# Layer 0's query and key maxima carried through the pairs as one sequence of steps, half a pair ahead

## What is computed

```python
q = (x @ Wq).reshape(B, Nq, HEADS, DIM_HEAD)
k = (context @ Wk).reshape(B, context.shape[1], HEADS, DIM_HEAD)
v = (context @ Wv).reshape(B, context.shape[1], HEADS, DIM_HEAD)
sim = jnp.einsum('bihd,bjhd->bhij', q, k) * SCALE
attn = jax.nn.softmax(sim, axis=-1)
out = jnp.einsum('bhij,bjhd->bihd', attn, v)
...
x = _layernorm(x + _L0_xattn_ref(x, ctx_768, ...), axis=-1)
```

## Time and profile before

| | us |
|---|---|
| median of 3 runs | 1639.53 (1639.24 to 1639.96) |
| the profiled execution | 1638.51 |
| its span | 1636.8 |
| maxima ahead of the pairs, first matmul to the reduction | 59.6 to 125.1 |
| half 0, seeds to seeds | 126.8 to 234.8 |
| half 1 | 234.8 to 358.9 |
| half 2 | 358.9 to 466.3 |
| half 6 | 821.6 to 912.1 |
| mean granted clock of TensorE | 0.964 |

### The profile page before, as it was taken

The page is one execution under the profiler, slowest core; times in us unless marked ns, Lnnn a source line. Parts: engine busy times, 40 slices in busy tenths (PEclk is TensorE's granted clock), DMA queues, the critical chain, the costliest instruction groups (busy, mean ns, idle before and its releaser), DMA issues.

```text
span 1636.8 us, 27033 instructions
## 1 busy us (share of the span) xinstructions
PE 1530.1 (93%) x9058; PEld 548.9 (34%) x9058; DVE 1286.3 (79%) x2319; ACT 1126.0 (69%) x1541; POOL 490.9 (30%) x488
## 2 busy tenths in 40 slices
PE   6889999999999999999999998899997979999986
PEld 4312333333333333333333223344444612222223
DVE  6898987879977779878789897877775666787766
ACT  6787777768877778777777786655554469676643
POOL 6303343334543334433300010345451012233100
PEclk9759999999999999999999998999999979999998
DMA  4000000000200000000010000111100000000000
GB/s 135 7 1 11 1 1 1 1 2 11 54 1 2 1 1 1 3 1 11 20 32 3 1 1 19 37 46 45 45 27 1 1 1 2 0 1 1 1 14 13
DMA packets 14834, 22.79 MB, mean 14 GB/s; under 512 B 1990, under 2 KB 11766, under 8 KB 14710
## 3 DMA queue, kind: packets, MB, share of 16 engines
q1 hardware_dynamic: 14710, 21.22, 4.6%
HBM read 20.69 MB, written 0.52 MB: 13 GB/s over the span
## 4 chain that ended last, share of the span: by engine, by line
PE 69%; issue 11%; DVE 9%; POOL 5%; ACT 4%; DMA 0%; POOLq 0%; SPq 0%; DVEq 0%; ACTq 0%
PE PS L2167 22%; PE PS L2153 15%; PE PS L2511 6%; PE PS L2199 5%; POOL WRK L734 5%; PE PS L2498 3%; DVE KNB L1382 3%; PE PS L2020 2%; PE PS L2012 2%; PE PS L2116 2%; PE PS L2540 2%; PE PS L2450 1%; PE PS L2435 1%; PE PS L2004 1%; ACT KNB L959 1%
## 5 line engine op out<-in xcount | busy, mean ns | idle before, releaser
L1382 DVE CUSTOM_DVE_ANT_0 KNB<-PS,KNB 128x512 f16<-128x512 f32 (+2 forms) x500 | 338.5, 690 | 152.4 <-PE PS L2199 106.9
L1432 DVE TENSOR_TENSOR WRK<-WRK 128x768 f32<-128x768 f32 (+3 forms) x400 | 425.2, 1063 | 15.3 <-ACT WRK L933 8.4
L933 ACT ACTIVATE WRK<-PS 128x1024 f32<-128x1024 f32 (+1 forms) x408 | 401.4, 1022 | 47.6 <-PE PS L2153 39.2
L2167 PE MATMUL PS<-WRK,V 128*64 128x512 f32 (+1 forms) x1632 | 395.7, 605 | 0.0
L708 POOL TENSOR_TENSOR WRK<-WRK 128x256 f32<-128x256 f32 x300 | 274.7, 916 | 395.6 <-ACT WRK L933 394.6
L959 ACT ACTIVATE KNB<-PS 128x512 f16<-128x512 f32 (+2 forms) x306 | 180.9, 591 | 77.8 <-PE PS L2199 77.2
L2344 PE MATMUL PS<-WRK,KNB 128*128 128x512 f16 x828 | 188.3, 381 | 7.1 <-POOL WRK L734 2.7
L2167 PEld LDWEIGHTS PS<-WRK,V 128*64 128x64 f32 (+1 forms) x1632 | 99.3, 136 | 192.7 <-issue 154.5
L2153 PE MATMUL PS<-KNB,KB 64*128 64x512 f16 (+1 forms) x1224 | 156.5, 377 | 0.0
L2153 PE MATMUL PS<-Q,KB 64*128 64x512 f16 (+1 forms) x1224 | 153.0, 377 | 0.0
L1162 ACT ACTIVATE WRK<-PS 128x1024 f32<-128x1024 f32 x100 | 102.4, 1024 | 51.1 <-PE PS L2498 47.6
(11 more groups left out here) (379 smaller groups left out, 1834.2 us busy)
## 6 DMA issues: line engine op xcount, KB each, us to landing
V<-in_moe_w_dram SPq DMA_DIRECT2D x44, 192.0 KB, 2.4
KNB<-in_ctx_fm_dram SPq DMA_DIRECT2D x6, 384.0 KB, 8.4
X<-in_ctx_fm_dram SPq DMA_DIRECT2D x12, 192.0 KB, 2.4
CTX<-in_ctx_fm_dram SPq DMA_DIRECT2D x6, 384.0 KB, 3.9
BW<-in_bit_w_dram SPq DMA_DIRECT2D x1, 960.0 KB, 9.8
PWK<-in_pair_w_dram SPq DMA_DIRECT2D x4, 192.0 KB, 2.8
XT<-in_x_fm_dram SPq DMA_DIRECT2D x1, 512.0 KB, 5.0
X<-in_x_tm_dram SPq DMA_DIRECT2D x1, 512.0 KB, 12.0
```

Of the source, the lines that this page charges most:

```text
L933: e.activation(PR[0:r, u % 2, b, :], bank(2 * b, 2 * b + 2, slice(0, r)), ACT.Exp).then_inc(S("exp"), 1)
L1382: return e.tensor_tensor_reduce(diffs, sums, diffs, 0.5, NEG, ALU.add, ALU.max, accum_out=out)
L1432: e.tensor_tensor(total, total, part, ALU.add).then_inc(S("acc"), 1)
L2167: ins = e.matmul(PS[h * HD:(h + 1) * HD, 4, :], V[0:r, j, h * HD:(h + 1) * HD], PR[0:r, unit_no(hf, i) % 2, b, h * HALF:(h + 1) * HALF], s ...
```

## The change

The maxima become one sequence over all pairs. Only those of half 0 are still made ahead (26 steps of up to 1024 columns). Those of halves 1 to 7 are 7 times 52 steps (`NSTEP` = 364), two a slot from slot 0 of pair 0 on, with a third one in nine slots of pairs 0, 1 and 2 (`WITH_VALUES`) and in three more of pair 0. They run past the end of pair 2 into the slots 0 to 11 of pair 3. Half by half, a half's last few columns are now 4 steps (before 6 for both halves of a pair).

In a slot of three steps the middle one stands behind both tiles' scores, on ScalarE behind both exponentials, on VectorE behind both sums. In a slot with a "v" item the last one follows the values' projection; in the others it stands between the two tiles of `values`.

`shifts` now does a half at a time, with its diagonals, as VectorE's first work in the last slot of the half before (slots 25 and 51). The queries and K16 of the next pair all go through bank 5, in other slots. GpSimd's share of the sums ends with half 5, but for units 3 to 11 of half 6. In the chain, `EMB[0]` lies in another buffer and the first projection waits for the last step.

```diff
+TILES_H = NT // 2
+STEPS = [[(c, [t], g) for c in range(NFULL) for t in range(TILES_H * u, TILES_H * u + TILES_H) for g in range(2)]
+         + [(NFULL, list(range(TILES_H * u + a, TILES_H * u + b)), g) for a, b in ((0, 3), (3, TILES_H)) for g in range(2)] for u in range(2)]
...
+POOL_HALVES = 2 * PAIRS - 2
+POOL_LAST = range(3, 12)
...
-THIRD_M = (32, 36, 40, 44, 48)
...
+NSTEP = NM * (2 * PAIRS - 1)
+WITH_VALUES = (32, 34, 36, 38, 40, 42, 44, 48, 50)
+THIRD_M = [(3, 4, 5) + WITH_VALUES] + [WITH_VALUES] * (PAIRS - 2) + [()]
...
+def first_step(p, s):
+    return min(2 * (p * SLOTS + s) + sum(len(x) for x in THIRD_M[:p]) + sum(t < s for t in THIRD_M[p]), NSTEP + 1)
...
+K16_AT = (6, 9, 13, 16, 20, 23, 25)
...
-        at[0] += [("wk", n), ("q", (n, 0)), ("q", (n, 1))]
-        at[1] += [("wv", n), ("kd", (n, 0)), ("ks", (n, 0))]
...
+        at[1] += [("wv", n), ("q", (n, 0))]
+        at[2].append(("q", (n, 1)))
...
-                    magnitude(p, first)
+                    first, mid, last = split_steps(p, s)
+                    magnitude(first)
                     exp(hf, i, 0)
-                    magnitude(p, mid)
                     for x in filter(inside, ITEMS[p][s]):
                         bank5(x)
                     if len(tiles_of(i)) > 1:
                         exp(hf, i, 1)
-                    magnitude(p, last)
+                    magnitude(mid)
+                    magnitude(last)
...
-                    if s == SLOTS - 1 and p + 1 < PAIRS:
-                        shifts(micro_base(p + 1), NMC, 2 * NT)
-                        e.wait_ge(S("sc"), tile_no(2 * p, 0, 0) + 1)
-                        diagonals(0, 2, NT)
+                    if i == NU - 1 and hf + 1 < 2 * PAIRS:
+                        shifts(hf + 1, STEP0 + (hf + 1) * NM, NMC)
...
-                if p + 1 < PAIRS:
-                    e.wait_ge(S("sc"), tile_no(2 * p + 1, 0, 0) + 1)
-                    diagonals(1, 2, NT)
...
-                    max_steps(p, first)
+                    max_steps(first)
                     scores(hf, i, 0)
-                    max_steps(p, mid)
                     for x in filter(inside, ITEMS[p][s]):
                         bank5(x)
                     if len(tiles_of(i)) > 1:
                         scores(hf, i, 1)
+
+                    max_steps(mid)
+                    makes_values = any(x[0] == "v" for x in ITEMS[p][s])
                     for x in ITEMS[p][s]:
                         if x[0] == "v" and mid:
                             bank5(x)
-                    max_steps(p, last)
+                    if makes_values or not mid:
+                        max_steps(last)
...
                         for b in tiles_of(before[1]):
                             values(*before, b)
+                            if b == 0 and mid and not makes_values:
+                                max_steps(last)
```

More of the change, by code:

```diff
@@ L93, in rows_of, with micro_steps, half_step, step @@
     return P if j < KT - 1 else TAIL
-THIRD_M = (32, 36, 40, 44, 48)
-def micro_steps(s):
-    if not FIRST_M <= s <= LAST_M:
-        return []
-    a = 2 * (s - FIRST_M) + sum(t < s for t in THIRD_M)
-    return list(range(a, a + 2 + (s in THIRD_M)))
-assert micro_steps(LAST_M)[-1] == NM
-def split_steps(s):
-    steps = micro_steps(s)
-    return steps[0:1], steps[1:-1], steps[-1:]
+NSTEP = NM * (2 * PAIRS - 1)
[3 more added lines that the diff above has]
+    return min(2 * (p * SLOTS + s) + sum(len(x) for x in THIRD_M[:p]) + sum(t < s for t in THIRD_M[p]), NSTEP + 1)
+def micro_steps(p, s):
+    return list(range(first_step(p, s), first_step(*divmod(p * SLOTS + s + 1, SLOTS))
+                      if p * SLOTS + s + 1 < PAIRS * SLOTS else NSTEP + 1))
+def half_step(m):
+    return 1 + m // NM, m % NM
+def step(m):
+    h, k = half_step(m)
+    return STEPS[h % 2][k]
+assert all(first_step(*divmod(h * NU - 1, SLOTS)) > h * NM for h in range(1, 2 * PAIRS))
+def split_steps(p, s):
+    steps = micro_steps(p, s)
+    return steps[:1], steps[1:-1], steps[1:][-1:]
 def inside(x):
     return x[0] == "dk"
-def micro_base(p):
-    return len(ALONE0) + NM * p
+STEP0 = len(ALONE0)
+K16_AT = (6, 9, 13, 16, 20, 23, 25)
 def items_of(p):
@@ L187 @@
 RELOAD = sorted(range(NKC), key=values_before)
-CHAIN = [("none",)] * 2
+CHAIN = [("none",)] * 3
 for _l in range(3):
@@ L1398, in max_alone, with shifts @@
                     ins.then_inc(S("mx"), 1)
-            def shifts(done, parts, rows):
+            def shifts(hf, done, parts):
+                u, rows = hf % 2, slice(hf % 2 * NT, hf % 2 * NT + NT)
                 e.wait_ge(S("mx"), done)
-                link(e.tensor_reduce(NEGM[:, 0:rows], MXP[:, 0:rows, 0:parts], X, ALU.max, negate=True))
-            def diagonals(u, heads, head_rows):
-                for h in range(heads):
-                    row = h * head_rows + 4 * u
+                link(e.tensor_reduce(NEGM[:, rows], MXP[:, rows, 0:parts], X, ALU.max, negate=True))
+                if hf >= 2:
+                    e.wait_ge(S("sc"), tile_no(hf - 2, 0, 0) + 1)
+                for h in range(2):
+                    row = u * NT + h * TILES_H
                     ins = e.tensor_tensor(DIAG[:, h, 4 * u:4 * u + 4, :],
@@ L1414, in _ @@
             max_alone(0, ALONE0, True)
-            shifts(len(ALONE0), NDC, 2 * NT)
-            for u in range(2):
-                diagonals(u, 2, NT)
+            shifts(0, STEP0, NDC)
             def add_up(hf, i, b):
                 n, r = tile_no(hf, i, b), rows_of(2 * i + b)
-                w = dve_part(hf)
+                w = dve_part(hf, i)
                 part = PR[0:r, unit_no(hf, i) % 2, b, 0:w]
@@ L2191, in project_out, with max_half @@
                 ins.then_inc(S("wo_ps"), 1)
-            def max_half(p, m, off, b, name):
-                c, tiles, g = STEPS[m]
+            def max_half(m, off, b, name):
+                c, tiles, g = step(m)
+                queries = QH[half_step(m)[0] // 2 % 2]
                 a, w = MCH[c]
@@ L2265, in _ @@
                     hf, i = 2 * p + s // NU, s % NU
-                    first, mid, last = split_steps(s) if p + 1 < PAIRS else ([], [], [])
+                    first, mid, last = split_steps(p, s)
                     if i == 0:
```

144 lines of the change are left out of this document (77 added, 67 removed).

## The result

The changed kernel took 1654.27 us (median of 4 runs, 1652.56 to 1656.72), the kernel before 1639.42 (4 runs, 1639.24 to 1639.96). The ratio is 1.0087, its interval 1.0071 to 1.0103: 0.9% slower. The forecast was 1651.5. The profiled execution of after took 1656.72 us (span 1655.0), the longest of its four, and that of before 1638.51. The traces therefore differ by 18.2 us where the medians differ by 14.9.

The account below looks back on a forecast made before the run. TensorE, busy 93% of the span, was taken as the bound, except in the VectorE-paced stage of maxima. Terms -31.6 + 11.0 + 23.5 + 6.9 + 3.0 = +12.8 us gave 1651.5 us, 0.7% slower; range 1644 to 1660.

Parts of the forecast that it names:

- Part 1: Stage of maxima ahead of the pairs, paced by VectorE, is halved: gain 31.6 us, the surest term.
- Part 2: Steps moved beside the slots of the pairs, 48 at 0.215 us of TensorE plus short ones: cost 11.0 us.
- Part 3: Slots of three steps: last step waits for the middle magnitude behind both exponentials, slot takes 5.81 us; cost 23.5 us.
- Rival 1: Three-step slots: magnitude's new place costs no more than the old wait, 6.7 instead of 23.5; about 1634.5 us, chance 0.15.
- Part 4: Shifts in a half's last slot delay the first maximum on VectorE, at six half ends: cost 6.9 us.
- Part 5: Steps in pair 3, where VectorE also has roundings and reciprocals and exceeds TensorE's slot: cost 3.0 us.
- Part 6: Queries and first K16 chunk through bank 5, at no cost; -3 to +3 us for gaps at a pair's start.
- point of decision: Three-step slot: the middle magnitude must be done by 2.5 us into the slot for the new place to cost nothing more.
- Rival 2: Half ends and pair 3 are hidden, costing zero there: 1641.5 us, within 0.2%; chance 0.13.
- Rival 3: VectorE becomes the bound where maxima, sums, rounding and shifts meet: about 1661 us; chance 0.11.
- Rival 4: TensorE's clock falls to half over 27 slots of the pairs through new gaps: some 1750 us; chance 0.03.

Follow-up runs that it names:

- the version with the magnitude alone: Changed kernel with only the middle step's magnitude moved back between the slot's two exponentials on ScalarE: 1634.24 us, ratio 0.9975.
- the early table load: Changed kernel with a one-column exponential on ScalarE right behind the maxima ahead of the pairs, loading its table there: 1652.17 us, ratio 1.0078.

## Why the prediction was right

**The sum, point by point.**

- *Part 1, -31.6:* measured -32.95. The seeds start at 93.88. Right; the gain was 1.3 larger.
- *Part 2, +11.0 for the steps' work:* halves 2 and 4 have no three-step slots and grew by 1.83 each. Their four more steps make 4 x 0.215 = 0.86, and the wait at the half's end (up to 0.9 in after) the rest. Right.
- *Part 3, +23.5:* the slot was laid out at 5.81 us with its last step at 3.61; it took 5.80 with the last step at 3.61. Moving the magnitude back gave 20.0 us of time, measured from a better slot than the old one; with the old slot restored whole it was 13.3, where the slots of 5.80 and 5.23 make 15.4. The halves 1, 3 and 5, where the slots stand, grew by 8.9 to 9.6 us as forecast. This term decided the sign and was right in size and mechanism. Its split was off a little: the listed wait is 0.93 and not the 1.115 that the prediction called idle, since the third step's own work is more than 0.215 (under *Rival 1*).
- *Part 4, +6.9:* too large. The waits at the six ends are 0.46 to 0.91 us, 4.1 in all, where I said 1.15 each; moving the shifts gave some 3 us. At the end of half 0 the diagonals even took 2.05 us where I had 1.40, and still TensorE waited only 0.86. VectorE had more to give than the 0.44 of the one slot that I took for all.
- *Part 5, +3.0:* about right. The steps' waits for VectorE in half 6 are 1.7 us, and the half grew by 7.0: 22 steps at 0.215 make 4.7 and leave 2.3.
- *Part 6, 0:* no sign of a cost. What TensorE waited for in the halves were magnitudes and maxima, not items, but for one wait of 0.91 us for an item in half 0 that the kernel before has as well.
- *Not in the sum:* the start of half 0, some 4 us. Half 0 grew by 9.8, and the terms give it about 5.5. I had listed the magnitudes that ScalarE gets and not what stood ahead of them in its first slot: a table load and two exponentials, with TensorE's wait of 2.37 and, in that execution, a clock that fell again. The load is 0.26 of the 4 us and the clock some 1.5; I did not take the remaining 2.5 apart. These 4 us too little and Part 4's 3 us too much nearly cancel (the 4 are those of the profiled execution, which took 2.5 us more than the median), so 1651.5 against 1654.3 looks better than its parts: the sign and Part 3 are no luck, the closeness is in part.

**The rivals.** *Rival 1* (the new place costs no more than the old wait) fell with the wait of 0.93 in eight slots of half 1 and of 0.66 in the ninth. It named the right lever. That its 1634.5 is also the time of the version with the magnitude alone (1634.24) is luck: its sum took the old slot of 5.23 us for all thirty, and the version with that slot measured 1641.0. Its point of decision was placed a little early. I had TensorE at its last step by 2.5 us; by its own list it is there at 1.51 + 0.33 + 0.77 = 2.61, and the maximum holds it until 2.82. The 0.535 of waiting that the prediction saw in the old slot was mostly not a wait. The old slot's one wait is the 0.25 for the maximum, ahead of the middle step. Its last step, with the magnitude and the reading of the maximum before it:

```profile
265.42 0.59 ACT L959 ACTIVATE KNB<-PS 128x512 f16<-128x512 f32 x1
...
265.97 0.08 DVE L1382 DVE_READ_ACCUMULATOR2_ANT MXP<- 128x1 f32 x1
...
266.47 0.39 PE L2199 MATMUL PS<-KNB,Q 64*128 64x512 f16 x2
```

It started 0.50 us behind the reading and 1.05 behind the magnitude, where 0.23 and 0.70 would do. So it was held by neither, and 0.50 of the third step's 0.75 was TensorE's own work in that order. The forecast of 5.81 did not hang on this, because ScalarE sets that slot. *Rival 2* (1641.5) fell with the waits at the halves' ends. *Rival 3* (1661) needed VectorE at its upper bounds; half 6 waited for it 1.7 us and not 7. *Rival 4*, the clock: in half 1 of after, with its gaps of 0.93 us, the clock was full:

```profile
211.66:344.72 133.06, 122.55 (x844) 45.01 (x842) 98.75 (x203) 95.46 (x140) 44.46 (x51) 1.00 0.01 1
829.99:927.47 97.48, 95.75 (x604) 31.54 (x602) 88.00 (x137) 75.68 (x92) 20.72 (x20) 1.00 0.03 7
```

(columns: window, length, busy of PE, PEld, DVE, ACT, POOL, clock, DMA share, GB/s; half 1, half 6). The rule about groups of matmuls with short idle times between them that the prediction cited from the Trainium skill (TensorE: Matmul & The Clock Gate, A second HAM failure mode: psum-queue depth-cycling) thus had no effect at this size of gap: 1.00 in this stretch. The one place in these halves where the clock did fall again is the start of half 0, behind the 2.37 us of idle time, at a cost of some 1.5 us. Likewise the two exponentials stand 1.83 us ahead of the magnitude (243.21 - 241.38), 0.91 each, so the measured pace and not the 1.15 of the Trainium skill's budget gives the slot.

**Still open:** whether the early table load has any part in the clock of the executions, beyond the 0.26 us that it saves; why the clock in the unchanged rest differs between executions; and some 2.5 of the 4 us at the start of half 0.

## What to carry over

When a step moves past a long instruction, do it engine by engine: here the same step gained 0.21 us a slot by standing later on TensorE, which makes it, and lost 0.78 by standing later on ScalarE, which frees its bank. Lay such a slot out from starts in the trace (exponentials at 1.09, magnitude at 2.91, step at 3.61); it came out to 0.01 us. And where work is put into a slot that had none, read each engine's first instructions there: a table load that nobody waited for came to stand in the path. Its price is the change in when the waiting step starts, 0.26 us, and not the change in the wait beside it, 1.14: a wait also shrinks when the engine that waits comes later.

## What of the hardware was unexpected

- A step can be held by another engine though the profile lists no idle time. In the three-step slots of 5.01 us the last step started 0.23 behind the reading of a maximum each time, 0.21 later than TensorE's own list allowed, with no wait listed. The constant distance between the two starts shows it.
- TensorE's clock at the start of half 0 differed in like executions. In after it was full from 98 to 100 us, fell behind 2.37 us of idle time and was 0.50 from 102 to 104 us, where TensorE was busy for all of it; in the version with only the shifts later it was full from some 101 us on and stayed so. The version with the magnitude alone ran from 1632.03 to 1639.61 us, with mean clocks of 0.975 down to 0.968; before, with its longer stage, ran from 1637.55 to 1643.38 in 21 executions beside it. So differences of 2 us between such versions are read from the slots, not from a few times.
- The table load takes 1.28 us and stands directly ahead of the first exponential in ScalarE's list, wherever that is: before it was hidden only because no magnitude came first.
